# Small VectorE steps dealt out between scans, the second norm one gap earlier, and the next convolution at the end of TensorE's slot

## What is computed

```
mod = (silu(c) @ wmod).reshape(8, 6, 1, 128); sa, ca, ga, sb, cb, gb = mod      # ga, gb: |.| at least 0.25
h = layernorm(x) * (1 + ca) + sa
# Mamba: d_inner 256, 16 states, rank 8, causal convolution of 4 taps
xz = h @ in_proj.T; u = silu(conv(x_part) + conv_b)
dt, B, C = split(u @ x_proj.T); delta = softplus(dt @ dt_w.T + dt_b)
state[t] = state[t-1] * exp(delta * A) + delta * u * B;  y = sum_n state * C + u * D
x = x + ga * ((y * silu(z)) @ out_proj.T)
h = layernorm(x) * (1 + cb) + sb
# experts: 8, of 256, the best 2 by softmax(h @ router_w + router_b), and one shared
x = x + gb * (shared(h) + sum_e weight_e * expert_e(h))
```

## Time and profile before

| | |
|---|---|
| median of 3 runs | 685.6 us (685.33 to 688.16) |
| profiled execution | 684.8 us, span 683.1 us |
| TensorE matmuls busy | 593.3 us (87%) |
| VectorE busy | 598.3 us (88%) |
| ScalarE busy | 489.7 us (72%) |
| POOL busy | 320.2 us (47%) |
| chain that ended last | TensorE 53%, VectorE 31%, issue 7%, ScalarE 5% |
| mean TensorE clock granted | 0.955 |

### The profile page before, as it was taken

One profiled execution on the slowest core, in us unless ns is written; L12 is line 12 of the kernel. 1 busy time (PEld: TensorE's weight loads), 2 busy tenths in 40 slices (PEclk: granted clock), 3 DMA queues, 4 the chain that ended last, 5 costly groups with the idle time before them and its releaser, 6 DMA issues.

```text
span 683.1 us, 9767 instructions
## 1 busy us (share of the span) xinstructions
PE 593.3 (87%) x3646; PEld 466.5 (68%) x3646; DVE 598.3 (88%) x713; ACT 489.7 (72%) x861; POOL 320.2 (47%) x171
## 2 busy tenths in 40 slices
PE   5684478899989998999989998999979947998897
PEld 4243345689657965788567966787668936798686
DVE  5399999999999999999999999999998999798416
ACT  3689535999589976989589957998598925962460
POOL 1036556446654556446653656446543664464000
PEclk9787589999999999999999999999999968999999
DMA  7423333314432235133531343223522442220000
GB/s 221 161 92 140 123 139 142 125 70 169 163 128 82 108 128 184 62 124 124 173 124 63 124 160 138 83 103 124 179 103 70 176 156 83 103 78 16 1 1 16
DMA packets 26705, 77.87 MB, mean 114 GB/s; under 512 B 3025, under 2 KB 17570, under 8 KB 18466
## 3 DMA queue, kind: packets, MB, share of 16 engines
q1 hardware_dynamic: 26178, 76.82, 31.1%
q10 hardware_dynamic: 480, 0.43, 0.2%
HBM read 74.61 MB, written 2.62 MB: 113 GB/s over the span
## 4 chain that ended last, share of the span: by engine, by line
PE 53%; DVE 31%; issue 7%; ACT 5%; POOL 2%; DMA 1%; DVEq 0%; POOLq 0%; ACTq 0%
DVE state L1206 15%; PE psum L677 12%; PE psum L516 10%; DVE psum L1197 8%; PE psum L543 5%; PE psum L645 5%; PE psum L647 4%; PE psum L646 4%; PE psum L687 3%; POOL state L433 2%; PE psum L662 2%; PE psum L565 1%; ACT L866 1%; DVE out_sb L1244 1%; PE psum L799 1%
## 5 line engine op out<-in xcount | busy, mean ns | idle before, releaser
L433 POOL TENSOR_TENSOR state<-state,bc 128x1024 f32<-128x1024 f32 x127 | 300.1, 2363 | 291.8 <-DVE psum L1197 291.8
L1206 DVE TENSOR_TENSOR_SCAN state<-decay,psum 128x1024 f32<-128x1024 f32 x128 | 292.2, 2283 | 21.9 <-PE psum L516 9.5
L885 ACT ACTIVATE decay<-delta,a_neg 128x511 f32<-128x511 f32 x256 | 166.1, 729 | 10.4 <-DVE state L1206 10.3
L516 PE MATMUL psum<-ident,state 128*128 128x128 f32 x1024 | 139.0, 283 | 33.6 <-POOL state L433 33.4
L1197 DVE TENSOR_TENSOR psum<-bc,du 128x1024 f32<-128x1024 f32 x128 | 157.6, 1231 | 4.8 <-DVE state L1206 0.5
L516 PEld LDWEIGHTS psum<-ident,state 128*128 128x128 f32 x1024 | 120.3, 146 | 56.0 <-POOL state L433 44.9
L677 PE MATMUL psum<-down_w,h 128*128 128x128 f32 x896 | 109.9, 276 | 0.0
L677 PEld LDWEIGHTS psum<-down_w,h 128*128 128x128 f32 x896 | 104.4, 192 | 5.3 <-issue 5.3
L1014 ACT ACTIVATE h<-psum,vec 128x512 f32<-128x512 f32 x144 | 97.0, 688 | 2.1 <-PE psum L647 0.6
L980 ACT ACTIVATE gT_mix<-psum,w 128x128 f32<-128x128 f32 x224 | 64.8, 388 | 20.0 <-PE psum L687 14.4
L645 PE MATMUL psum<-h_hi,up_hi 128*128 128x512 f32 x144 | 59.2, 411 | 10.7 <-DVE h_lo L1310 6.7
(11 more groups left out here) (151 smaller groups left out, 638.3 us busy)
## 6 DMA issues: line engine op xcount, KB each, us to landing
bc<-bc_rows SPq DMA_DIRECT2D x64, 1024.0 KB, 4.7
x_sb<-_attn_hidden_states_dram SPq DMA_DIRECT2D x9, 256.0 KB, 2.8
x<-_attn_hidden_states_dram SPq DMA_DIRECT2D x7, 256.0 KB, 3.0
out_dram<-out_sb SPq DMA_DIRECT2D x7, 256.0 KB, 2.4
h<-in_L_ffn_rw_dram SPq DMA_DIRECT2D x1, 1024.0 KB
bc_rows<-rows SPq DMA_DIRECT2D x8, 64.0 KB, 4.8
h<-in_L_wmod_dram ACTq DMA_DIRECT2D x1, 384.0 KB
h<-in_L_attn_in_proj_w_dram SPq DMA_DIRECT2D x1, 256.0 KB, 4.7
```

What stands on the lines that cost most here:

```text
L433: pool.tensor_tensor(state[:, u % STATE_RING, :, :], state[:, u % STATE_RING, :, :], bc[:, pair % BC_RING, 1, first:first + NU, :], ALU.mu ...
L516: last = nc.tensor.matmul(Y[q][:, t * P:(t + 1) * P], state[:, u % STATE_RING, s, t * P:(t + 1) * P], ident[:, :], start=False, stop=(u in ...
L885: last = nc.scalar.activation(decay[:, r, s, 1:L], delta[:, b.p, q, 1:L], ACT.Exp, scale=a_neg[:, q, k:k + 1])
L1206: nc.vector.tensor_tensor_scan(state[:, u % STATE_RING, :, :].rearrange("p n t -> p (n t)"), decay[:, u % DECAY_RING, :, :].rearrange("p n ...
```

## The change

- **VectorE.** The small steps are split into functions of one or a few instructions and dealt out, one group to nearly every gap and pause between scans (`scan_slots`). `finish` of a batch moves from gap 15 to behind scan 0 of the next slot. `residual` and its statistics (`stats2`) move from gap 3 to behind scan 2, x1hat from behind scan 3 to gap 3, logits from behind scan 4 to gap 4. The statistics of the first norm get a tile of their own, are taken one slot earlier in gaps 12 to 15, and x is loaded that much earlier.
- **Ranking.** A probability is compared with another one times 1 or (1 - 2^-24) instead of with is_equal, a mask and an add: seven instructions instead of nine.
- **TensorE.** `conv_in` of the next batch goes from the start of a slot to the end of the one before, around the last `mix_add`; `z_proj` goes ahead of the last `y_add` of the old batch; y_add 2 to 4 go between the up-projections; fillers 14 and 5 become 24 and 10; `x_transpose` moves ahead of the third down block.
- **ScalarE.** `h_rows` from j = 6 to j = 3; decays 3 and 4 of the next batch ahead of `acc_rows`.
- **POOL.** The second rstd comes ahead of readout 2, which now waits for x1hat; the first rstd comes at the start of the slot.
- **SyncE.** The output store and the residual load go to the next slot; x's load is one slot earlier.

```diff
@@ sync: slots @@
-                if m and first_batch:
+                if m and not b and n:
                     sp.wait_ge(xT_done, m.i)
                     load_x(m)
+                if a and a.i > 0:
+                    store(Batch(a.i - 1, 1 - a.p))
+                if a:
+                    load_residual(a)
...
-                if m and n and not first_batch:
-
-                    load_x(m)
                 if b:
                     load_bc(b, 2)
                     load_bc(b, 3)
-                if n:
-                    load_bc(n, 0)
+                if b and m and m.i + 1 < B:
+                    sp.wait_ge(xT_done, m.i + 1)
+                    load_x(Batch(m.i + 1, 1 - m.p))
...
+                if n:
+                    load_bc(n, 0)
                     load_bc(n, 1)
@@ gpsimd: slots @@
+                if m and (a or not b):
+                    make_rstd(0, stats_done, rstd_eps, rstd_done, m)
                 for u in range(UN - 1):
+                    if a and u == 2:
+                        make_rstd(1, stats2_done, rstd2_eps, rstd2_done, a)
+                        pool.wait_ge(xhat2_done, a.i + 1)
                     if b:
                         readout(b, u)
-                    if a and u == 2:
-                        make_rstd(1, stats2_done, rstd2_eps, rstd2_done, a)
-                    if m and u == 5:
+                    if m and b and not a and u == 1:
                         make_rstd(0, stats_done, rstd_eps, rstd_done, m)
@@ tensor: conv_in, slots @@
+                if n.i >= 3:
+                    pe.wait_ge(mixmul_done, DOWNS * (n.i - 2) - 1 + q)
...
-                if n:
+                if n and not a:
                     conv_in(n, 0)
-                if a:
-                    y_add(a, UN - 4)
-                if n:
                     conv_in(n, 1)
                 if a:
                     y_add(a, UN - 3)
-                    y_add(a, UN - 2)
...
                 if a:
-                    y_add(a, UN - 1)
+                    y_add(a, UN - 2)
                 if n and n.i > 0:
                     z_proj(n, 0)
                     z_proj(n, 1)
+                if a:
+                    y_add(a, UN - 1)
                 if a:
                     g_transpose(a, n)
...
                 if a:
-                    keep_busy(a, n, 14)
+                    keep_busy(a, n, 24)
                     x1_transpose(a)
-                if b:
-                    y_add(b, 2)
-                if a:
-                    keep_busy(a, n, 5 if b else 12)
+                    keep_busy(a, n, 10)
                     router(a)
-                    for k in range(M_UP):
+                for k in range(M_UP):
+                    if a:
                         up(a, n, k)
-                if b:
-                    y_add(b, 3)
+                    if b and k in (2, 8, 14):
+                        y_add(b, 2 + (k - 2) // 6)
                 if a:
                     weights_transpose(a)
-                if b:
-                    y_add(b, 4)
...
+                    if m and u == 8:
+                        x_transpose(m, n, a)
                     for j in MIX_AT[u]:
                         if a and j + 2 < DOWNS:
                             down(a, j + 2)
-                        if a:
+                        if a and j < DOWNS - 1:
                             mix_add(a, j)
-                    if m and u == 10:
-                        x_transpose(m, n, a)
                     if b and u < UN - 3:
                         y_add(b, u - 1)
+                if b and m:
+                    conv_in(m, 0)
+                if b:
+                    y_add(b, UN - 4)
+                if a:
+                    mix_add(a, DOWNS - 1)
+                if b and m:
+                    conv_in(m, 1)
                 if a:
                     acc_transpose(a)
@@ vector: ranking @@
-                nc.vector.tensor_tensor(gt_eq[:, 1, :, :, :], other, mine, ALU.is_equal
-                                        ).then_inc(prob_step, 1)
-                nc.vector.tensor_tensor(gt_eq[:, 0, :, :, :], other, mine, ALU.is_gt
-                                        ).then_inc(prob_step, 1)
...
+            def tie_bars(a):
+                dve.wait_ge(prob_step, 6 * a.i + 3)
                 nc.vector.tensor_tensor(
-                    gt_eq[:, 1, :, :, :], gt_eq[:, 1, :, :, :],
-                    before[:, :, :].unsqueeze(1).broadcast_to([P, NT, E, E]),
+                    gt_eq[:, 1, :, :, :], pr[:, :, :].unsqueeze(3).broadcast_to([P, NT, E, E]),
+                    tie_scale[:, :, :].unsqueeze(1).broadcast_to([P, NT, E, E]),
                     ALU.mult).then_inc(prob_step, 1)
```

More of the change, by code:

```diff
@@ L806, in tail @@
             def tail(a):
-                for u in range(UN - 4, UN - 1):
+                for u in range(UN - 3, UN - 1):
                     y_add(a, u)
@@ L1073, in slots @@
                     mix_scaled(a, DOWNS - 1)
+                if n:
+                    decays(n, 3)
+                    decays(n, 4)
+                if a:
                     acc_rows(a)
                 if n:
-                    for u in range(3, AHEAD):
-                        decays(n, u)
+                    decays(n, 5)
             def tail(a):
@@ L1319, in slots @@
                 if b:
-                    scan_input(b, 0)
-                    scan(b, 0)
-                    scan_input(b, 1)
+                    scan_slots(b, a, n, m)
+                    return
+                if m:
+                    for t in range(NT):
+                        bn_x(m, t)
+                    nc.vector.memset(pace, 0.0)
+                    aggr_x(m)
+                    for t in range(NT):
+                        xhat(m, t)
+                if n:
+                    split_up_weights()
+                    relu_plus_exp(n)
+                    rounded_exp(n)
+                    minus_rounded(n)
+                    for q in range(Q):
+                        plus_log(n, q)
+                    delta_x(n)
@@ new lines, in scan_slots @@
+            def scan_slots(b, a, n, m):
+                late = Batch(m.i + 1, 1 - m.p) if m and m.i + 1 < B else None
+                new = m if b.i == 0 else None
+                old = m if b.i > 0 else None
+                scan_input(b, 0)
+                if new:
+                    bn_x(new, 0)
+                    bn_x(new, 1)
+                if old:
+                    aggr_x(old)
+                scan(b, 0)
+                if a and a.i > 0:
+                    finish(Batch(a.i - 1, 1 - a.p))
+                scan_input(b, 1)
+                if new:
+                    bn_x(new, 2)
+                    bn_x(new, 3)
@@ L1323, in slots @@
                 if a:
                     gate_y(a)
-                if b:
-                    scan(b, 1)
-                    scan_input(b, 2)
-                    scan(b, 2)
-                if b:
-                    scan_input(b, 3)
+                scan(b, 1)
+                if old:
+                    xhat(old, 0)
+                    xhat(old, 1)
+                scan_input(b, 2)
+                if new:
+                    aggr_x(new)
+                if old:
+                    xhat(old, 2)
@@ L1363, in slots @@
-                for u in range(8, UN):
-                    if b:
-                        scan_input(b, u)
-                    if a:
-                        if u == UN - 1:
-                            finish(a)
-                    if b:
-                        scan(b, u)
-                    if n and u == 12:
-                        delta_x(n)
+                scan(b, 4)
+                if new:
+                    xhat(new, 0)
+                    xhat(new, 1)
+                    xhat(new, 2)
@@ new lines, in scan_slots @@
+                scan_input(b, 5)
+                if m:
+                    xhat(m, 3)
+                scan(b, 5)
+                if a:
+                    prob_sum(a)
+                if n:
+                    relu_plus_exp(n)
+                if a:
+                    prob_inverse(a)
+                scan_input(b, 6)
+                if a:
+                    probs(a)
+                scan(b, 6)
+                if a:
+                    tie_bars(a)
+                    beaten(a)
+                scan_input(b, 7)
@@ new lines, in scan_slots @@
+                if a:
+                    ranks(a)
+                scan(b, 7)
+                if a:
+                    weights(a)
+                scan_input(b, 8)
+                scan(b, 8)
+                if n:
+                    rounded_exp(n)
+                scan_input(b, 9)
+                if n:
+                    minus_rounded(n)
+                scan(b, 9)
+                scan_input(b, 10)
+                if n:
+                    plus_log(n, 0)
+                scan(b, 10)
@@ new lines, in scan_slots @@
+                scan_input(b, 11)
+                if n:
+                    plus_log(n, 1)
```

(18 more changed lines are left out.)

142 lines of the change are left out of this document (72 added, 70 removed).

## The result

The changed kernel takes 715.1 us (median of 4 runs, 712.2 to 717.8), the one before 685.5 beside it: ratio 1.042, 95% interval 1.037 to 1.048. It is slower, as forecast, but by 30 us where 9 were forecast, and 4 us beyond the end of the range. The profiled execution took 712.2 us (684.8 before).

The account below looks back on a forecast made before the run. TensorE was taken to bound the slot, 77.85 us instead of 75.05: 14.0 over five slots, less 1.5, 3.1 and 0.3 elsewhere, is 9.1, which on 685.6 gives about 695 us, range 679 to 711.

Parts of the forecast that it names:

- What bounds, and the sign: TensorE bounds the five equal slots, each 2.8 us longer; VectorE, needing some 70 us, waits some 3 at each gate.
- the second as nothing, since a step of 32 elements so close behind may still get in: VectorE's L1260 in gap 4, arriving 0.3 us after readout 3 started: held 0 us, bounds 0 to 2.1.
- The first meeting: POOL's first rstd step arrives inside VectorE's input 3, before x1hat: held the full 1.2 us, bounds 0 to 1.2.
- the rival's walk: Both meetings cost in full: weights 2.1 us more, shared_down at +37.0, slot 80.05, 710 in all; chance 0.26.
- SP's store and residual load come one slot later with 10 us to spare: SyncE's output store and residual load, issued one slot later, still come with 10 us to spare.
- z_proj ahead of the gate, 1.73: z_proj, moved from beside gate_y to before the gate, adds 1.73 us to TensorE's stretch from shared_down to gate.
- shared_down to gate, 43.05: TensorE's stretch from shared_down to the next gate: 41.57 - 1.14 + 1.73 + 0.15 + 0.74 = 43.05 us.
- The weights: Router weights ready at +33.5 after the gate: TensorE waits 1.0 us, then 1.3 uncovered until shared_down.
- The meetings cost nothing: Rival: neither meeting holds a step; x1hat at +11.95, shared_down at +33.85, slot 76.9, 686 in all; chance 0.21.
- faster: Rival: meetings cost nothing and VectorE's dealt steps run shorter, so both TensorE waits go, 7.2 for five slots: 679; chance 0.17.
- Other slots: Outside the five equal slots: first -1.5 us, the one without a next convolution -3.1, last -0.3, tail order kept.

Follow-up runs that it names:

- once the weights were covered: Kernel with both edits, delta's first 1.2 us step put behind the router weights and y_add 4 behind their transposes: 683.2 us, 0.995 of the kernel before.
- SyncE's queue clear: Kernel with the weights covered, SyncE's write and broadcast of the last gate row moved from batch 1's slot to the last: 679.4 us, 0.988.
- the kernel with both edits: Changed kernel, readout 3 held until the logits are done and z_proj put back behind the last y_add: 692.0 us, 1.006 of the kernel before.

## Why the prediction was wrong in size

- **What bounds, and the sign: right.** TensorE ends the slot, VectorE waits at the gates from the second to the sixth (4.51 us; 3 forecast), and VectorE's relief, from 71.5 us to 68.6 of its own, shortens no slot of this kernel.
- **The step that failed: "the second as nothing, since a step of 32 elements so close behind may still get in".** Reading it by how near it starts was the error; the measured rule is who starts first. L1284 starts 0.27 us behind readout 3 and takes 2.16 us. Taking that away gives 17 us of the 30 (715.1 to 697.9), 3.1 us in each equal slot: 2.0 of hold, and the clock. By the ratios, each beside its own measurement of the kernel before (1.042 and 1.016), it is 18 us. The first meeting, taken in full (1.2), held its step by 0.9.
- **A term that stood in no case: the clock.** The longer wait, 2.68 us, is followed by some 3 us at 1.2 GHz and 1.5 us of later up-projections in four of the five slots. This, not VectorE, is why shared_down came at +37.4 there: the weights were ready at g+34.75 (L1322 starts at 464.68 and takes 0.17), 0.9 earlier than in the rival's walk, and TensorE came for them at +35.8. In the slot where the clock stayed up it came at +36.15.
- **"SP's store and residual load come one slot later with 10 us to spare": wrong in one slot.** I looked at the usual slot, not at the one with the gate row in SyncE's queue: 1.7 us of wait in the changed kernel, 4.3 once the weights were covered.
- **z_proj ahead of the gate, 1.73: right.** Swapping it back shortens the wait at the gate by exactly that, and three slots by 1.6 to 1.9, where 1.5 was forecast.
- **shared_down to gate, 43.05: right** (43.0), and so are its parts. In the changed kernel's order of time L705 waits for nothing, z_proj takes 1.73 (507.70 to 509.43), and x_proj starts 0.10 late (0.15). The mixes cost 0.70 where 0.74 was forecast: the last two down blocks start 0.43 and 0.27 us later than the pitch of the matmuls before them, the first of them with this wait for ScalarE:

```profile
488.24 2.05 PE L686 MATMUL psum<-down_w,h 128*128 128x128 f32 x16 [0.27 <-ACT gT_mix L991]
```

- **The weights: right as a mechanism, half the size.** Where neither meeting nor clock covers it, the wait before their transposes is 0.52 us (1.0 forecast) and the one behind them 0.77; covering both gave 0.9 us a slot. With the meeting out the weights are ready at g+32.8 (33.5 forecast).
- **"The meetings cost nothing" at 686, "faster" at 679: not this kernel.** But the mechanism of the faster case is what the edits built: with the second meeting out, z_proj back, the weights covered and SyncE's queue clear, 679.4 was measured. That it is the same number is luck: the faster case kept z_proj ahead of the gate and had no cost for the first meeting.
- **Other slots:** the first came as forecast (-1.3); the one without a next convolution gained 1.0 instead of 3.1, and the last lost 1.4 where -0.3 was forecast, both near the dear rival's figures. The tail keeps its order and was 1.4 us longer, with a granted clock of 0.83 in ten of its microseconds where it was 1.00 before. In five kernels of the experiments with this tail it took 53.4 us with the clock up at that place, in two others 54.9 with the clock down; what sets it off is open.

With the second meeting in full, the case at 710 was the one to name. That its slot of 80.05 came so near the measured 80.40 is partly luck: it had the weights 0.9 us too late and the clock at nothing, and where the clock stayed up the slot was 79.15. What lies between 710 and 715.1: 1.8 us in the five slots (the load's 1.7 is in them), 1.4 in the tail, -0.5 in the other stretches, and the 2.2 us that no profile shows. The clock may have a part in those. Times of one kernel go with the mean granted clock in the kernel with both edits (above) and in 29 executions of the kernel before: 688.0 to 691.6 us at 0.943 or less, 683.4 to 688.3 at 0.952 or more. But the four executions of the changed kernel, at 0.942 to 0.947, don't line up this way (717.8 us at 0.947, 712.2 at 0.946), so for the 2.2 us it is not shown.

## What to carry to other kernels

When small steps are dealt into the gaps of a paced pair of engines, list for each step with two SBUF inputs, and for each tensor_scalar, what the other engine has started by then: a 0.19 us step behind a 2.36 us one costs the long one's remainder, whatever its own size. Moving work past a wait asks two questions, what it now covers and who was queued behind the old place: the convolution cost 2.4% until `finish` moved as well. A one-off transfer in an in-order queue is harmless until something urgent is put behind it.

## What the runs showed of the hardware beyond that

- **GpSimd's duration in the trace includes the time it is held.** Its readouts average 2363 ns when paced, 2503 in the changed kernel and 3026 without pacing, so a longer readout is a sign of a meeting, not of more work. Which side paid is read from both engines: the step that cost this kernel its time (L1284) shows in VectorE's rows alone, and taking it away leaves the readouts' mean at 2504.
- **The clock falls after the wait, not in it, and what sets it off stays open.** In the slot shown the granted clock stays at 1.00 through the 2.68 us wait and 1 us on, then 0.59 and 0.50 for 3 us with TensorE fully busy. In the changed kernel and in the one with z_proj moved back the fall follows this wait (2.60 to 2.68 us) in eight of the nine slots that have it, and it comes at this place in none of the five with the meeting taken out, where the wait is 0.64 to 0.70. But the clock also falls without a long wait before it: in the kernel with both edits at g+9 of one slot, where TensorE's last wait had been 0.24 us, and not in the next one with the same order. The pair gives the price, 1.4 us:

```profile
263.45:340.40 76.95, 73.96 (x463) 58.80 (x462) 69.36 (x78) 61.51 (x111) 43.71 (x20) 0.98 0.34 122
340.40:415.97 75.57, 72.50 (x463) 57.11 (x462) 69.42 (x77) 61.51 (x111) 43.66 (x20) 1.00 0.35 122
```
